# A graph and expert kernel: indirect loads of 127 rows instead of 128, edge steps of 508 columns, 108 blocks a layer

## What is computed

```
h = relu(conv(layernorm(x), Wq1..bs1));  h = relu(conv(h, Wq2..bs2))
x = x + sigmoid(h @ Wo.T + bo)
x = x + sum_e softmax(mean(layernorm(x)) @ Wr + br)[e] * expert_e(layernorm(x))   # 8 experts, 3 products each

conv: q, k, v = x @ W.T + b, as 4 heads of 16
      logits = (q[dst] * k[src]).sum(-1) / 4
      e = exp(logits - segment_max(logits, dst)[dst])
      out = segment_sum(v[src] * e) / (segment_sum(e) + 1e-16) + x @ Ws.T + bs
```

## Time and profile before

| | |
|---|---|
| median of 3 runs | 3700.6 us |
| profiled execution, span | 3707.0 us |
| TensorE busy | 2464.8 us (66%) |
| VectorE busy | 2398.1 us (65%) |
| GpSimd busy | 2051.4 us (55%) |
| ScalarE busy | 1119.3 us (30%) |
| kv gathers, first and last start | 197.1 and 2665.7 us |

### The profile page before, as it was taken

One profiled execution on the slowest core, in us unless ns is written; L12 is line 12 of the kernel. 1 busy time (PEld: TensorE's weight loads), 2 busy tenths in 40 slices (PEclk: granted clock), 3 DMA queues, 4 the chain that ended last, 5 costly groups with the idle time before them and its releaser, 6 DMA issues. The chain is left out here.

```text
span 3707.0 us, 49221 instructions
## 1 busy us (share of the span) xinstructions
PE 2464.8 (66%) x13243; PEld 2115.8 (57%) x13243; DVE 2398.1 (65%) x3615; ACT 1119.3 (30%) x2130; POOL 2051.4 (55%) x1958
## 2 busy tenths in 40 slices
PE   2435556665656656265656556655569999999999
PEld 1324444554545444154544444444459989989898
DVE  3347777777777764277777777777746556566555
ACT  6301111111111111011111111111146666666665
POOL 6567777777777747677777777777610000000000
PEclk9756666666666655566666666666679999999999
DMA  9334444444444422344444445444310000000000
GB/s 378 112 103 119 125 121 122 125 119 128 119 127 119 124 69 71 87 123 136 124 129 127 125 125 132 124 131 125 97 38 4 23 22 3 23 22 2 21 11 11
DMA packets 394181, 356.62 MB, mean 96 GB/s; under 512 B 88694, under 2 KB 327436, under 8 KB 394080
## 3 DMA queue, kind: packets, MB, share of 16 engines
q1 hardware_dynamic: 221360, 168.40, 15.2%
q0 software_dynamic: 62896, 125.63, 13.6%
q10 hardware_dynamic: 109824, 61.36, 5.4%
HBM read 246.90 MB, written 108.30 MB: 96 GB/s over the span
## 5 line engine op out<-in xcount | busy, mean ns | idle before, releaser
L542 POOL DMA_INDIRECT kv<-kv_table,ix x1664 | 1786.4, 1074 | 531.4 <-issue 497.2
L554 PE MATMUL kT<-identity,kv 128*128 128x128 f32 x832 | 361.3, 435 | 1037.6 <-DMA kv<-kv_table,ix 1037.6
L554 PEld LDWEIGHTS kT<-identity,kv 128*128 128x128 f32 x832 | 182.5, 219 | 1061.1 <-DMA kv<-kv_table,ix 813.4
L650 ACT ACTIVATE ex<-gap 128x1024 f32<-128x1024 f32 x208 | 219.8, 1057 | 1859.4 <-DVE gap L626 1859.4
L604 DVE TENSOR_TENSOR_SCAN held_q<-mask,held_q,qT 128x512 f32<-128x512 bf16 x208 | 266.1, 1280 | 600.4 <-PE qT L555 599.5
L1324 DVE TENSOR_TENSOR hid_lo_x<-full_x,hid_hi_x 128x448 fp32r<-128x448 f32 x448 | 276.2, 622 | 267.8 <-ACT hid_hi_x L1210 264.0
L1210 ACT ACTIVATE full_x<-psH_x,offset_x,scale_x 128x448 f32<-128x448 f32 x448 | 332.5, 742 | 290.6 <-PE psH_x L1065 290.5
L561 PE MATMUL logit<-kq,head_sum 128*128 128x512 f32 x416 | 388.7, 1037 | 1.9 <-DVE gap L626 1.9
L1014 POOL DMA_DIRECT2D x_x<-in_x x7 | 6.8, 974 | 633.6 <-DVE total_x L1368 633.6
L555 PE MATMUL qT<-identity,qz 128*128 128x128 f32 x832 | 347.2, 417 | 0.0
L578 PE MATMUL restT<-pick,top 128*128 128x8 f32 x1664 | 335.4, 274 | 0.0
(11 more groups left out here) (209 smaller groups left out, 5238.8 us busy)
## 6 DMA issues: line engine op xcount, KB each, us to landing
running_sums<-rows ACTq DMA_DIRECT2D x208, 288.0 KB
qz<-q_at_starts SPq DMA_DIRECT2D x208, 256.0 KB, 3.2
mask<-masks SPq DMA_DIRECT2D x416, 128.0 KB, 3.7
q_at_starts<-zeros SPq DMA_DIRECT2D x16, 1664.0 KB, 18.7
kv<-kv_table,ix POOLq DMA_INDIRECT x1664
x_sb<-in_x SPq DMA_DIRECT2D x1, 6272.0 KB, 27.3
kv_table<-proj SPq DMA_DIRECT2D x14, 448.0 KB, 3.3
x_x<-in_x POOLq DMA_DIRECT2D x7, 896.0 KB, 5.7
```

Of the source, the lines that this page charges most:

```text
L542: pool.indirect_dma_start(kv[:, u, j, 2 * HC * s:2 * HC * (s + 1)], None, kv_t, bass.IndirectOffsetOnAxis(ix[:, u, n:n + 1], 0), bounds_ch ...
L554: pe.transpose(kT[u % 2][:, P * j:P * (j + 1)], kv[:, u, j, 0::2], identity[:, :])
```

## The change

A row tile of the edge phases has 127 partitions instead of 128 (`ROWS`). The step is 4 x 127 = 508 edges a stream, so a layer needs 108 blocks (27 turns) instead of 104 (26 turns); three turns are peeled instead of two, and the loop keeps its 24. `ix`, `kv`, `qz` and `rows` have 127 partitions, and their four kinds of DMA with them. The table of zeros is rounded up to a multiple of 128 rows. The transpositions become 127 wide, and the turned results keep a pitch of 128 in PSUM.

```
-STEP = 512
-TPB = STEP // P
+ROWS = 127
+TPB = 4
+STEP = TPB * ROWS
 UNROLL = 4
 BLOCKS = -(-E // (STREAMS * STEP * UNROLL)) * UNROLL
...
+QROWS = -(-EP // P) * P
...
-assert STEPS - 2 == len(EXPERT_LAYERS) * EXPERTS
+PEELED = STEPS - len(EXPERT_LAYERS) * EXPERTS
+assert PEELED >= 2
...
-    qz_blocks = qz_t.rearrange("(b j p s) c -> b p j (s c)", j=TPB, p=P, s=STREAMS)
-    sum_blocks = sum_t.rearrange("(b j p s) c -> b p j (s c)", j=TPB, p=P, s=STREAMS)
+    qz_blocks = qz_t[0:EP, :].rearrange("(b j p s) c -> b p j (s c)", j=TPB, p=ROWS, s=STREAMS)
+    sum_blocks = sum_t.rearrange("(b j p s) c -> b p j (s c)", j=TPB, p=ROWS, s=STREAMS)
...
-            zeros = sb("zeros", [P, EP * HC // P // 32])
+            zeros = sb("zeros", [P, QROWS * HC // P // 32])
...
-                ix = sb("ix", [P, U, TPB * STREAMS], I32)
-                kv = sb("kv", [P, U, TPB, STREAMS * 2 * HC])
-                qz = sb("qz", [P, U, TPB, STREAMS * HC])
+                ix = sb("ix", [ROWS, U, TPB * STREAMS], I32)
+                kv = sb("kv", [ROWS, U, TPB, STREAMS * 2 * HC])
+                qz = sb("qz", [ROWS, U, TPB, STREAMS * HC])
...
-                rows = sb("rows", [P, 2, TPB, STREAMS, ROW])
+                rows = sb("rows", [ROWS, 2, TPB, STREAMS, ROW])
...
-                peeled = 2
+                peeled = PEELED
...
-                            pe.transpose(kT[u % 2][:, P * j:P * (j + 1)], kv[:, u, j, 0::2], identity[:, :])
+                            pe.transpose(kT[u % 2][:, ROWS * j:ROWS * (j + 1)], kv[:, u, j, 0::2], identity[0:ROWS, 0:ROWS])
...
-                            pe.transpose(outT[:, of], run_v[:, u, of], identity[:, :])
+                            pe.transpose(outT[0:ROWS, P * j:P * (j + 1)], run_v[:, u, of], identity[:, :])
...
-        "src": np.ascontiguousarray(src.reshape(STREAMS, BLOCKS, TPB, P).transpose(1, 3, 2, 0).reshape(BLOCKS, P, TPB * STREAMS)),
+        "src": np.ascontiguousarray(src.reshape(STREAMS, BLOCKS, TPB, ROWS).transpose(1, 3, 2, 0).reshape(BLOCKS, ROWS, TPB * STREAMS)),
```

More of the change, by code:

```diff
@@ L93, in build @@
     q_t = nc.dram_tensor("q_table", [NP, HC], F32, kind="Internal").ap()
-    qz_t = nc.dram_tensor("q_at_starts", [EP, HC], F32, kind="Internal").ap()
+    qz_t = nc.dram_tensor("q_at_starts", [QROWS, HC], F32, kind="Internal").ap()
     sum_t = nc.dram_tensor("running_sums", [EP, ROW], F32, kind="Internal").ap()
     mask_t = nc.dram_tensor("masks", [STREAMS, BLOCKS, 2 * STEP], BF16, kind="Internal").ap()
-    qz_blocks = qz_t.rearrange("(b j p s) c -> b p j (s c)", j=TPB, p=P, s=STREAMS)
-    sum_blocks = sum_t.rearrange("(b j p s) c -> b p j (s c)", j=TPB, p=P, s=STREAMS)
+    qz_blocks = qz_t[0:EP, :].rearrange("(b j p s) c -> b p j (s c)", j=TPB, p=ROWS, s=STREAMS)
+    sum_blocks = sum_t.rearrange("(b j p s) c -> b p j (s c)", j=TPB, p=ROWS, s=STREAMS)
     kv_nodes = kv_t.rearrange("(i p) c -> p i c", p=P)
@@ L241, in _ @@
                             sp.dma_start(mask_t[s], mask_b[:, s, :, :].rearrange("b m c -> b (m c)")).then_inc(masks_out, 16)
-                    sp.dma_start(fill[m], zeros[:, :].unsqueeze(1).to_broadcast([P, 32 // FILLS, EP * HC // P // 32])).then_inc(filled[m % len(filled)], 16)
+                    sp.dma_start(fill[m], zeros[:, :].unsqueeze(1).to_broadcast([P, 32 // FILLS, QROWS * HC // P // 32])).then_inc(filled[m % len(filled)], 16)
                 store_tables(sp, projected, GROUP, stored)
@@ L452, in pb @@
                 def pb(name):
-                    return phase.enter_context(nc.psum_tensor(f"{name}_{layer}", [P, STEP], F32))
+                    return phase.enter_context(nc.psum_tensor(f"{name}_{layer}", [P, 512], F32))
                 U = UNROLL
-                ix = sb("ix", [P, U, TPB * STREAMS], I32)
-                kv = sb("kv", [P, U, TPB, STREAMS * 2 * HC])
-                qz = sb("qz", [P, U, TPB, STREAMS * HC])
+                ix = sb("ix", [ROWS, U, TPB * STREAMS], I32)
+                kv = sb("kv", [ROWS, U, TPB, STREAMS * 2 * HC])
+                qz = sb("qz", [ROWS, U, TPB, STREAMS * HC])
                 mask = sb("mask", [P, U, 2, STEP], BF16)
@@ L473, in edge_phase @@
                 vT, logit, outT = pb("vT"), pb("logit"), pb("outT")
-                restT = pb("restT")[:, 0:2 * TPB * STREAMS * HEADS].rearrange("p (m j h) -> p m j h", m=2, j=TPB)
+                restT = pb("restT")[0:ROWS, 0:2 * TPB * STREAMS * HEADS].rearrange("p (m j h) -> p m j h", m=2, j=TPB)
                 block = phase.enter_context(nc.Block())
                 past = STEPS * layer
-                peeled = 2
+                peeled = PEELED
                 def each_step(eng, body):
@@ L553, in turn_kq @@
                         for j in range(TPB):
-                            pe.transpose(kT[u % 2][:, P * j:P * (j + 1)], kv[:, u, j, 0::2], identity[:, :])
-                            ins = pe.transpose(qT[u % 2][:, P * j:P * (j + 1)], qz[:, u, j, :], identity[:, :])
+                            pe.transpose(kT[u % 2][:, ROWS * j:ROWS * (j + 1)], kv[:, u, j, 0::2], identity[0:ROWS, 0:ROWS])
+                            ins = pe.transpose(qT[u % 2][:, ROWS * j:ROWS * (j + 1)], qz[:, u, j, :], identity[0:ROWS, 0:ROWS])
                         ins.then_inc(kq_turned, 1)
@@ L560, in logits @@
                         wait_past(pe, gaps_ready, b)
-                        pe.matmul(logit[:, :], head_sum[:, :], kq[:, u % 2, :], start=True, stop=True)\
+                        pe.matmul(logit[:, 0:STEP], head_sum[:, :], kq[:, u % 2, :], start=True, stop=True)\
                             .then_inc(logits_ready, 1)
@@ L566, in turn_v @@
                         for j in range(TPB):
-                            ins = pe.transpose(vT[:, P * j:P * (j + 1)], kv[:, u, j, 1::2], identity[:, :])
+                            ins = pe.transpose(vT[:, ROWS * j:ROWS * (j + 1)], kv[:, u, j, 1::2], identity[0:ROWS, 0:ROWS])
                         ins.then_inc(v_turned, 1)
@@ L574, in turn_results @@
                         for j in range(TPB):
-                            of = slice(P * j, P * (j + 1))
-                            pe.transpose(outT[:, of], run_v[:, u, of], identity[:, :])
+                            of = slice(ROWS * j, ROWS * (j + 1))
+                            pe.transpose(outT[0:ROWS, P * j:P * (j + 1)], run_v[:, u, of], identity[:, :])
                             pe.matmul(restT[:, 0, j, :], run_d[:, u, of], pick[:, :], start=True, stop=True)
-                            ins = pe.matmul(restT[:, 1, j, :], top[:, u, 1 + P * j:1 + P * (j + 1)], pick[:, :],
+                            ins = pe.matmul(restT[:, 1, j, :], top[:, u, 1 + ROWS * j:1 + ROWS * (j + 1)], pick[:, :],
                                             start=True, stop=True)
@@ L603, in hold_q @@
                         wait_past(dve, q_held, b)
-                        dve.tensor_tensor_scan(held_q[:, h, :], mask[:, u, 0, :], qT[h][:, :],
+                        dve.tensor_tensor_scan(held_q[:, h, :], mask[:, u, 0, :], qT[h][:, 0:STEP],
                                                held_q[:, 1 - h, STEP - 1:STEP], ALU.mult, ALU.add).then_inc(q_held, 1)
@@ L607, in hold_q @@
                         wait_past(dve, logits_ready, b - 1)
-                        dve.tensor_tensor(kq[:, h, :], kT[h][:, :], held_q[:, h, :], ALU.mult).then_inc(kq_ready, 1)
+                        dve.tensor_tensor(kq[:, h, :], kT[h][:, 0:STEP], held_q[:, h, :], ALU.mult).then_inc(kq_ready, 1)
                     def maximum(b, u, i):
@@ L617, in maximum @@
                         dve.wait_ge(logits_ready, b + 1)
-                        dve.tensor_tensor_scan(now, mask[:, u, 1, :], logit[:, :], last,
+                        dve.tensor_tensor_scan(now, mask[:, u, 1, :], logit[:, 0:STEP], last,
                                                ALU.add, ALU.max).then_inc(top_ready, 1)
@@ L623, in maximum @@
                         dve.tensor_tensor(gap[:, h, 1, :], before, now, ALU.subtract).then_inc(grown, 1)
-                        dve.tensor_tensor(gap[:, h, 0, :], logit[:, :], now, ALU.subtract).then_inc(grown, 1)
+                        dve.tensor_tensor(gap[:, h, 0, :], logit[:, 0:STEP], now, ALU.subtract).then_inc(grown, 1)
                         dve.wait_ge(grown, 2 * b + 2)
@@ L631, in sums @@
                         dve.wait_ge(v_turned, b + 1)
-                        dve.tensor_tensor(wv[:, h, :], vT[:, :], ex[:, h, 0, :], ALU.mult).then_inc(weighted, 1)
+                        dve.tensor_tensor(wv[:, h, :], vT[:, 0:STEP], ex[:, h, 0, :], ALU.mult).then_inc(weighted, 1)
                         wait_past(dve, out_turned, b - U + 1)
@@ L657, in store @@
                         flat = rows[:, h, :, :, :].rearrange("p j s c -> p (j s) c")
-                        act.activation(flat[:, :, 0:HC], outT[:, :].rearrange("p (r c) -> p r c", c=HC),
+                        act.activation(flat[:, :, 0:HC], outT[0:ROWS, 0:TPB * P].rearrange("p (r c) -> p r c", c=HC),
```

## The result

The changed kernel takes 8420.3 us (median of 4 runs, 8409.96 to 8439.09) against 3702.1 us: ratio 2.276, 95% interval 2.272 to 2.281. The forecast was 7,725 us within 7,000 to 9,500, and slower. The profiled execution has a span of 8437.4 us.

What follows compares the result with a forecast made beforehand. Before, GpSimd's kv gathers were taken to bound at 10.98 us a block; after, one full DMA ring at 29.0. 1423.4 + 216 x 29.0 (6264) + 42 = 7729, less 6: 7,725 us, range 7,000 to 9,500.

Steps and rivals of the forecast that it cites:

- One ring: SP and ACT queues: a DMA over 127 partitions goes on one ring; ACT's queue would show 109944 packets.
- One engine for both queues: SP's and ACT's single rings belong to the same DMA engine, 33.3 us a block before overlap; two-engines rival 0.08.
- The ring's price: Full single ring in the edge phases: 29.0 us a block taken, bounds 27.8 to 33.3; chance 0.70.
- DMA share and rate: Edge phases after: DMA share about a tenth to 0.2, GB/s from 122 to near 45.
- POOL's issue: GpSimd's issue of each kv gather: left at 1.07 us; POOL's block 7.0 to 18.6 us, covered by the ring's 29.
- POOL at three tenths: Sign for the page after: GpSimd is busy for only three tenths.
- TensorE waiting for qz and no longer for kv: Sign for the page after: TensorE, POOL and VectorE all wait, for qz first and no longer for kv.
- if POOL is still without idle time: Sign that the prediction is wrong: GpSimd still has no idle time after the change.
- The stalls rival: ACT, held by the full ring at its store, adds a chain of about 9 us: 38 us a block, 9,670 us; 0.12.
- The spread at the old price: 127 rows still spread over the rings, POOL's price unchanged: 216 x 10.98 = 2372, 3,790 us; chance 0.06.
- The faster one: 127 rows still spread, gather issue 0.57 us, VectorE bounding at 8.5 us a block: 3,255 us; chance 0.04.
- The sum: Whole kernel: 1423.4 + 216 x 29.0 (6264) + 42 = 7729, less 6: 7,725 us.

Runs made afterwards that it cites:

- e4: Kernel before, with only the store of the sums made two DMAs, over partitions 0 to 126 and over partition 127: 5197.5 us, ratio 1.319.
- e5: Kernel before, with only the qz load made two DMAs, over partitions 0 to 126 and over partition 127: 5014.0 us, ratio 1.36, a single run.
- e6: Kernel before, with both the store and the qz load made two DMAs, over partitions 0 to 126 and over partition 127: 7119.8 us, ratio 1.807.
- e8: Kernel before, with only its kv gathers cut to 127 rows: 7556.9 us, ratio 1.918.
- e3: Changed kernel, with gathers of 128 rows, and qz and the store each in two DMAs over 112 and 15 partitions: 4046.6 us, ratio 1.026.
- e1: Changed kernel, with qz, ix and the store each in two DMAs over partitions 0 to 111 and 112 to 126, gathers still 127 rows: 7817.0 us, ratio 1.983.
- e2: Changed kernel, with kv and ix of 128 partitions and gathers of 128 rows, qz and the store still at 127: 7326.2 us, ratio 1.858.
- e7: Kernel before, with a block's eight gathers at 128, 127, 126, 120, 112, 96, 64 and 16 rows: 4063.2 us.
- e11: Kernel before, with a block's eight gathers at 127, 125, 124, 122, 121, 113, 97 and 31 rows: 4953.8 us.
- e12: Kernel before, with all gathers cut to 113 rows in layer 0 and to 97 rows in layer 1: 6412.7 us.
- e10: Kernel before, with every second gather cut to 127 rows and the others at 128: 5026.1 us, ratio 1.36, a single run.

## Why the prediction was right, and where it was not

- **One ring.** Right. The count of completions before (612 instead of 624) foretold 109944 packets on the ACT queue to the packet.
- **One engine for both queues.** Right, though no row showed it then: e4, e5 and e6 show it (17.4 and 17.3 alone, 26.7 together).
- **The ring's price.** Right for the packets: store and qz were 14.8 + 14.2 = 29.0 us, less 4.8 ns for each of 1016 packets, 24.1 us; the trace has 508 x 49 ns = 24.9 us. With masks and gathers e6 has 26.7 us, and with 1.2 us for ix the ring by itself would take 27.9, the lower bound of the forecast (27.8) and not the 29.0 that I chose. The overlap that I took from a full stretch is there, but only where two rings have work.
- **DMA share and rate.** 0.21 and 44 GB/s, against "about a tenth to 0.2" (81 us in 16 x 29 is 0.17) and near 45 foretold. The rest of the share is about the small pieces: 8 x 240 of 15 ns are 29 us a block.
- **POOL's issue.** This is the step that failed: "If issuing to a single ring is cheaper or dearer, from 0.57 us (...) to 2.02 us (the longest gather) (...), POOL's block is 7.0 to 18.6 us; the ring's 29 us cover both. I leave the 1.07 us." It is 2.64 us, above the upper bound, and with a stall that no row before showed 29.3 us a block by itself (e8), as high as the ring. I had costed a row's price by rows (16 rows against 128) where the rows of a share count (1 against 8: the 0.1 us between them is 0.0134 us x 7), and had the rule of the shares in hand for the other queues. "POOL at three tenths" and "TensorE waiting for qz and no longer for kv" failed with it: POOL is busy for 66% of the stretch from 1000 to 3000 us. One of my own signs of being wrong, "if POOL is still without idle time", is met in substance, since its idle time is again "issue" but for 41.4 us.
- **The stalls rival.** Its mechanism, ACT held by the ring, is seen in e4 and not in the changed kernel, whose ACT issues a store in 0.22 us.
- **The other rivals.** The spread at the old price is 3,790 us: that is e3's kernel, 1.026. The faster one never had its condition.

The sum, counted as in the prediction (gathers and their "issue" alone): 29.0 us a block were forecast, (4568.8 + 2323.7)/216 = 31.9 us measured. 2.9 x 216 = 628 us and 80 us in the rest, half of it the 41.4 us of waits for ix, are the 708 us between 7729 and 8437.4. (The terms of the forecast give 7,723 and not 7,725 us.)

How the block of 32.1 us comes about is shown in part. The gathers alone, with the ordinary DMAs spread, take 29.5 us (e1), and the full ring adds 2.7 us to the pauses between gathers. The ring alone takes 26.7 us (e2). The rest of its load in the changed kernel is an estimate: ix adds 1.2 us (127 packets of 9 to 10 ns), and the small pieces about 1.5 us (of 8 gathers 7.5 on average leave 16 pieces on this ring, 120 x 15 ns less overlap), 29.4 us in all. So two bounds of nearly equal height stand side by side and cost more together than either. They do not meet through ix or the buffers, since GpSimd waited 41.4 us for the one and never for the other. Gathers and ordinary DMAs do share the engines, but that this is what lengthens GpSimd's pauses is argued and not shown.

So the forecast was right about the first bound, and the number came near by luck as well: the second bound, which I had at no more than 18.6 us, is as high as the first. Had only the gathers changed, my working would have given the time of the kernel before, and e8 has 7556.9 us beside 3941.8.

## What to carry to other kernels

Count the completion packets of SP's or ACT's queue before changing a tile's height: they tell over how many DMA rings a transfer is split, and a height without a divisor from 2 to 16 (127, 113, 97) puts all of it on one. An indirect DMA has 16 completions whatever its height (e7), so there the data packets and the small pieces tell. Ask the question for every issuing engine, for the indirect DMAs too, whose issue time grows with the rows on the fullest ring. And when a new bound is found that covers everything, still cost the others under the same rule: here two nearly equal ones stood side by side, and mending one of them brings the ratio to the kernel before from 2.28 only to 1.98 (e1) or 1.86 (e2), both together to 1.03 (e3).

## What the runs showed of the hardware

- An indirect load's issue on GpSimd takes 0.90 us + 0.0134 us for each row of a share: 1.00 us for 128 rows on 16 rings, 2.60 us for 127 rows on one, 1.31 us for 31 rows on one (e7, e11).
- A gather of 127 rows leaves 272 packets instead of 32, 240 of them of 28 to 32 B. The rule that each ring without a share gets 4 B for every row of one gives the packet counts of e7 and e11 exactly.
- Gathers of 127 or 113 rows in an unbroken row stall for some 6 us at every eighth; those of 97 rows don't, nor those of 127 and 128 rows in turn (e8, e12, e10). The cause is open.
- One queue alone on an engine moves a 576 B run every 29 ns and a 512 B run every 27 ns; two queues on it take turns one by one and move one of each in 49 ns (e4, e5, e6).
- A DMA issued behind 508 packets on one ring holds the issuing queue for about as long as they take to drain: 15.31 us on ACT (e4), 27.78 us for the two mask DMAs on SP (changed kernel).
